# Three extension pairs instead of one, an x ring of 14 pieces, and LoRA factors held for one batch

## What is computed

```python
# conditioning: a dense layer plus the LoRA of the batch's slot
A, Bm = lora_As[adapter_mapping], lora_Bs[adapter_mapping]
c = einsum('bti,oi->bto', x, W) + b + einsum('btr,bro->bto', einsum('bti,bir->btr', x, A), Bm) * 2
# mixture of 8 experts of rank 16, the best one chosen by the router
logits = c @ route_w.T
topk_v, topk_idx = top_k(logits, 1)
route_weight = one_hot(topk_idx) * topk_v
h = einsum('bsd,erd->bser', c, Aexp)
return x + einsum('bser,eor->bso', route_weight[..., None] * h, Bw)
```

## Time and profile before

| | us |
|---|---|
| median of 3 runs | 283.86 |
| the profiled execution | 284.19 |
| its span | 282.4 |
| PE busy | 277.1 (98%) |
| DVE busy | 200.7 (71%) |
| ACT busy | 110.3 (39%) |
| DMA, share of 16 engines by q1 | 76.1% |

### The profile page before, as it was taken

The page is one execution under the profiler, slowest core; times in us unless marked ns, Lnnn a source line. Parts: engine busy times, 40 slices in busy tenths (PEclk is TensorE's granted clock), DMA queues, the critical chain, the costliest instruction groups (busy, mean ns, idle before and its releaser), DMA issues.

```text
span 282.4 us, 4103 instructions
## 1 busy us (share of the span) xinstructions
PE 277.1 (98%) x1601; PEld 221.0 (78%) x1601; DVE 200.7 (71%) x223; ACT 110.3 (39%) x151; POOL 14.9 (5%) x46
## 2 busy tenths in 40 slices
PE   8999999999999999999999999999999999999993
PEld 5999999997773888888588758867885888588882
DVE  0033010177497889999889969996998799788794
ACT  0001011387684645534275346326533743370000
POOL 7600021000001000000000000000000000000000
PEclk9999999999999999999999999999999999999999
DMA  7999999999993034999966993999399859606688
GB/s 257 382 377 394 399 407 411 384 407 421 412 408 133 2 149 187 352 343 388 396 269 230 418 402 146 348 405 398 136 370 406 316 176 412 287 22 253 261 355 321
DMA packets 19590, 88.50 MB, mean 313 GB/s; under 512 B 2410, under 2 KB 4594, under 8 KB 12018
## 3 DMA queue, kind: packets, MB, share of 16 engines
q1 hardware_dynamic: 16272, 83.70, 76.1%
q10 hardware_dynamic: 3298, 4.54, 4.4%
HBM read 54.60 MB, written 33.55 MB: 312 GB/s over the span
## 4 chain that ended last, share of the span: by engine, by line
PE 93%; DVE 6%; issue 0%; DVEq 0%
PE bank_out L683 11%; PE bank_eh L811 11%; PE bank_eh L825 10%; PE bank_eh L840 10%; PE bank_out L749 9%; PE bank_out L772 9%; PE bank_out L763 9%; PE bank_eh L683 5%; PE bank_rl L683 5%; PE bank_rl L790 5%; PE bank_eh L790 5%; DVE x_ring L666 4%; PE bank_rl L721 1%; PE bank_eh L711 1%; PE bank_rl L845 1%; PE bank_eh L846 1%
## 5 line engine op out<-in xcount | busy, mean ns | idle before, releaser
L402 ACT ACTIVATE x_hi<-x_ring 128x1024 fp32r<-128x1024 f32 x64 | 67.4, 1061 | 57.7 <-PE bank_eh L840 57.3
L518 DVE TENSOR_TENSOR x_lo<-x_ring,x_hi 128x1024 fp32r<-128x1024 f32 x64 | 77.6, 1222 | 8.7 <-ACT x_hi L402 8.7
L607 DVE TENSOR_TENSOR x_ring<-bank_out,x_ring 128x1024 f32<-128x1024 f32 x54 | 65.9, 1220 | 2.9 <-PE bank_out L772 2.7
L811 PE MATMUL bank_eh<-x_hi,m_hi 128*128 128x512 f32 x128 | 50.6, 396 | 0.0
L825 PE MATMUL bank_eh<-x_lo,m_hi 128*128 128x512 f32 x128 | 49.9, 390 | 0.0
L840 PE MATMUL bank_eh<-x_hi,m_lo 128*128 128x512 f32 x128 | 49.8, 389 | 0.0
L749 PE MATMUL bank_out<-wh_hi,bw_hi 128*128 128x512 f32 x120 | 46.7, 389 | 0.0
L763 PE MATMUL bank_out<-wh_lo,bw_hi 128*128 128x512 f32 x120 | 46.7, 389 | 0.0
L772 PE MATMUL bank_out<-wh_hi,bw_lo 128*128 128x512 f32 x120 | 46.7, 389 | 0.0
L811 PEld LDWEIGHTS bank_eh<-x_hi,m_hi 128*128 128x128 f32 x128 | 24.0, 188 | 10.7 <-issue 5.9
L840 PEld LDWEIGHTS bank_eh<-x_hi,m_lo 128*128 128x128 f32 x128 | 24.0, 188 | 5.1
(11 more groups left out here) (99 smaller groups left out, 227.1 us busy)
## 6 DMA issues: line engine op xcount, KB each, us to landing
x_ring<-xT SPq DMA_DIRECT2D x32, 1024.0 KB, 8.4
outT<-x_ring SPq DMA_DIRECT2D x26, 1024.0 KB, 4.9
w_ring<-W SPq DMA_DIRECT2D x24, 512.0 KB, 10.6
w_ring<-W SPq DMA_DIRECT2D x14, 256.0 KB, 5.9
outT<-x_ring SPq DMA_DIRECT2D x5, 512.0 KB, 2.8
outT<-x_ring ACTq DMA_DIRECT2D x4, 512.0 KB, 2.8
outT<-x_ring SPq DMA_DIRECT2D x5, 256.0 KB, 2.7
x_ring<-loraB ACTq DMA_DIRECT2D x8, 128.0 KB, 9.9
```

The costliest lines, as they stand in the source:

```text
L402: act.activation(out, in_, ACT.Copy).then_inc(done, 1)
L518: dve.tensor_tensor(out, a, b, ALU.subtract).then_inc(done, 1)
L607: dve.tensor_tensor(x, out_bank(b, j)[:, :, :], x, ALU.add).then_inc(v_out, 1)
L811: mm(bank_h, m_hi[:, c, :], hi, start=(c == 0), stop=False)
```

## The change

1. `TWINS = range(2, 7, 2)`: extensions 2, 4 and 6 now run straight after extensions 1, 3 and 5. ACT, DVE and PE treat 4 and 6 as they treated 2; PE's waits that belong to them move to the end of the batch two before.
2. `XRING` is 14 and `LAG` is 1: after `store(k)` comes `load_x(k + 13)`, which waits until store k - 1 has landed.
3. `la` holds one batch. Each `load_a(b)` waits until GpSimd has copied the factor before (`g_ext`); `load_a(1)` and `load_a(2)` stand among the ACT work of phase 1, `load_a(b + 3)` behind the `wh_hi` copy of batch b, up to b = 4.
4. Room for the ring: `g_a`, `bp`, `pb_sum`, `ones` and `bias_sb` lie in slot 10 (`WORK`), whose first load waits for their last readers; `e_top`/`e_two` and `e_odd`/`e_sum` share two tiles in different partitions. The two copies of `stack` change places.

```diff
-    XRING = 12
+    XRING = 14
...
+        TWINS = range(TWIN, NB - 1, 2)
...
                 if k >= XRING:
                     sp.wait_ge(d_out[slot], 16 * (k // XRING))
+                elif slot == WORK:
+                    sp.wait_ge(t_pb, 1)
+                    sp.wait_ge(v_glo, 3)
+                    sp.wait_ge(a_ghi, 6)
+                    sp.wait_ge(a_beats, 3)
...
-            LAG = 2
+            LAG = 1
...
             def load_ext(b):
-                if b == TWIN + 1:
-                    pool.wait_ge(d_la, 16 * (NB - TWIN - 1))
+                pool.wait_ge(d_la, 16 * (b + 1))
...
+            def load_a(b):
+                if b >= 1:
+                    act.wait_ge(g_ext, b)
+                act.dma_start(la[:, :, :].rearrange("p c r -> p (c r)"),
+                              loraA[bass.ds(slot[b], 1), :, :].rearrange("s p n -> p (s n)")).then_inc(d_la, 16)
...
                 copy(wh_hi[b % 2][:, :], wh[:, :], a_wh)
+                if b + 3 < NB:
+                    load_a(b + 3)
...
+                ext_last = b + 3 if b + 3 in TWINS else b + 2
...
-                        pe.wait_ge(g_ext, ext_next + 1)
+                        pe.wait_ge(g_ext, ext_last + 1)
...
-                    if (b, j, i) == (TWIN - 2, NP2 - 1, 1):
-                        pe.wait_ge(v_wh, TWIN)
+                    if b + 2 in TWINS and (j, i) == (NP2 - 1, 1):
+                        pe.wait_ge(v_wh, b + 2)
...
-                if b != TWIN:
+                if b not in TWINS:
                     extension(b)
-                if b + 1 == TWIN:
-                    extension(TWIN)
+                if b + 1 in TWINS:
+                    extension(b + 1)
```

More of the change, by code:

```diff
@@ L107, in adaln_ffn, with work @@
         x_ring = sb("x_ring", [P, XRING, PIECE])
-        lb = x_ring[:, 8, :].rearrange("p (b c r) -> p b c r", b=NB, c=C)
-        bw_raw = x_ring[:, 9, :]
+        lb = x_ring[:, 12, :].rearrange("p (b c r) -> p b c r", b=NB, c=C)
+        bw_raw = x_ring[:, 13, :]
         lb_cols = x_ring[:, 11, :].rearrange("p (c b r) -> p c b r", b=NB, c=C)
-        EARLY = (8, 9, 11)
+        EARLY = (11, 12, 13)
+        WORK = 10
+        def work(at, n, rows=P):
+            return x_ring[0:rows, WORK, at:at + n]
+        g_a = work(0, NB * XN, GROUP).rearrange("p (b n) -> p b n", b=NB)
+        bp = work(NB * XN, XN)
+        pb_sum = [work((NB + 1) * XN + i * PN, PN) for i in range(2)]
+        ones = work((NB + 1) * XN + 2 * PN, P)
+        bias_sb = work((NB + 1) * XN + 2 * PN + P, C)
+        assert (NB + 1) * XN + 2 * PN + P + C <= PIECE
         phase1 = ExitStack()
@@ L129, in adaln_ffn @@
         wh = sb("wh", [P, T])
[L130 to L136, removed]
+        assert (C - WO) * PN + NHEAD * (HEAD_W + HO * PN) + XN + 2 * E + P // 2 <= 7 * T, "the second lot covers the first"
+        e_st = sb("e_st", [P, T], F32R)
+        ahead = sb("ahead", [P, T], F32R)
+        e_bias = sb("e_bias", [P, 1])
         slots = sb("slots", [1, NB], I32)
+        sb("space", [P, HALF - 16])
         m_hi = sb("m_hi", [P, C, ER], F32R)
@@ L443, in _ @@
                     act.dma_start(g_a[BIAS_ROW:BIAS_ROW + 1, :, :], pb[:, :].unsqueeze(1).broadcast_to([1, NB, XN])).then_inc(d_g, 16)
+                    load_a(1)
                 if n == NWB - 2:
@@ L459, in _ @@
                         split_hi(0, j)
+                    load_a(2)
                 m_block(blk)
-            load_a(TWIN + 1, NB)
             def top(b):
@@ L479, in stack @@
                     act.wait_ge(t_stack, b)
+                copy(e_st[2 * GROUP:3 * GROUP, :], e_sum[:, :], a_ehi)
                 copy(e_st[0:GROUP, :], e_sum[:, :], a_ehi)
-                copy(e_st[2 * GROUP:3 * GROUP, :], e_sum[:, :], a_ehi)
             for b in range(NB):
-                if b != TWIN:
+                if b not in TWINS:
                     top(b)
                 for j in range(NP2):
-                    if j == 0 and b != TWIN:
+                    if j == 0 and b not in TWINS:
                         odd(b)
-                    if b + 1 == TWIN and j == 0:
+                    if b + 1 in TWINS and j == 0:
                         stack(b)
[L491 to L496, removed]
+                        top(b + 1)
+                    if b + 1 in TWINS and j == 1:
+                        odd(b + 1)
+                    if b + 1 in TWINS and j == TWIN_AT:
+                        stack(b + 1)
+                    if j == EHI_AT and b not in TWINS and b + 1 not in TWINS:
                         stack(b)
@@ L640, in _ @@
                         split_lo(b, SRING + j)
-                    elif b + 1 < NB and (b + 1, j) != (TWIN, NP2 - 1):
+                    elif b + 1 < NB and not (b + 1 in TWINS and j == NP2 - 1):
                         split_lo(b + 1, j - SRING)
@@ L742, in out_pair @@
                     pe.wait_ge(v_whlo, b + 1)
-                ext_next = b + 2 if j == NP2 - 1 and TWIN < b + 2 < NB else None
+                ext_next = b + 2 if j == NP2 - 1 and TWIN < b + 2 < NB and b + 2 not in TWINS else None
+                ext_last = b + 3 if b + 3 in TWINS else b + 2
                 hi, lo = wh_hi[b % 2][:, :], wh_lo[b % 2][:, :]
@@ L787, in extension @@
                             pe.wait_ge(v_m, NWB)
-                        if c == C - 1 and b > TWIN:
+                        if c == C - 1 and b > TWIN and b not in TWINS:
                             pe.wait_ge(v_wh, b)
```

58 lines of the change are left out of this document (24 added, 34 removed).

## The result

| | before | after |
|---|---|---|
| median of 6 runs | 283.87 us (283.49 to 284.16) | 288.88 us (288.06 to 289.87) |
| ratio, 95% interval | 1 | 1.0174 (1.0161 to 1.0188) |
| profiled execution | 284.19 us | 288.40 us, span 286.6 us |

A forecast was written before the change was run, and what follows sets the result against it. PE, busy 98% of the span, was taken to bound the kernel. On the profiled 284.19 us, -0.70 (pairs) + 2.3 + 1.2 (waits) = +2.8 us: 287.0 us profiled, 286.7 us median; range 283.1 to 288.6 us.

The forecast's parts named there:

- Late arrivals are paid in full: On PE, busy 98% of the span: whatever arrives late adds its whole delay, since PE has no idle time.
- A pair saves 0.35 us: On PE, two extensions back to back save one entry into and exit from the 32-column form; two new pairs save 0.70 us.
- First wait, 2.3 us: In extension 4, PE waits for x piece 19, landing at 144.0 us against a deadline of 141.76 us.
- its turn comes no later: Piece 19's load, issued 1.5 us later by the lag, stands behind store 6 either way, so no delay was added.
- Second wait, 1.2 us: In the pair of extensions 5 and 6, PE waits for piece 27; the middle between 0 and 2.3 us.
- The cause, one fetch packet that a full queue can't make good: A PE program fetch on queue q8 at 124 us delays the full DMA queue by 2.1 us; landings take 9.4, not 7.0.
- The factor load, 0.3 us: `load_a(5)`, 0.13 MB on ACT's queue, mixes packets with piece 19's load and makes it 0.3 us later.
- What costs nothing: Factor loads on ACT, copies at batch ends, slot 10's late first load and PE's waits for `v_wh` add no time.
- (a): Rival: all pieces in time, loads landing in 7.0 + 0.3 us, only the 0.70 us saving stays; 283.2 us, chance 20%.
- (b): Rival: only the fetch packet's own 1.3 us counts, landings near 8.0, waits 0.7 us in all; 283.9 us, chance 12%.
- (c): Rival: ACT held in phase 1 by `load_a(2)`, extension 0 waits some 1.2 us; 287.9 us on the forecast, chance 5%.
- (d): Rival: the late load is issued and lands later, waits 3.8 us at first pair, 2.3 at second; 289.3 us, chance 6%.

The follow-up runs named there:

- e3: The changed kernel, but extensions 4 and 6 read the x pieces of batches 3 and 5, already there, so the output differs; 283.08 us.
- e2: The changed kernel with only the pairs of extensions (1, 2) and (3, 4), without the pair (5, 6); 286.92 us.
- e1: The changed kernel with only the old pair, extensions 1 and 2; ring of 14, lag of 1 and factor loads stay; 283.91 us.
- e6: The changed kernel with LAG = 2, so every load comes one store later; 300.64 us.
- e5: The changed kernel with 96 extra PE instructions in phase 1 that wait for nothing, so the fetch packets fall elsewhere; 287.44 us.
- e8: The changed kernel without the factor loads of batches 3 to 7, whose extensions use factor 2, so the output differs; 287.12 us.
- e10: The changed kernel with factor loads half a batch later and 96 extra PE instructions in phase 1 that move the fetch packets; 286.11 us.
- e12: The changed kernel with factor loads half a batch later, loads 19 and 27 ahead of stores 6 and 14, and 96 extra PE instructions; 284.35 us.
- e9: The changed kernel with the factor loads issued half a batch later, same computation; 286.59 us.

## Why the prediction was off, point by point

- *Late arrivals are paid in full.* Right: +4.1 us by the losses, +4.2 measured between the profiled executions. Of the signs, the landings "over 9 us" came true for the first load only (9.3, then 8.5 and 8.7 us), since the others left later than I had them.
- *A pair saves 0.35 us.* Right: 52.11 us against 52.46 from pair A to pair B, 7.00 us per pair wherever nothing is late, and e3 is 0.8 to 1.0 us under the kernels with one pair.
- *First wait, 2.3 us.* Right to 0.1 (2.43), with luck in it. The load left at 135.75 and not 134.32, because it waited for store 5, as my upper end had it; and it took 8.7 us and not 9.7, because "its turn comes no later" was nearly right as well. It landed at 144.45, 0.45 us later than I had it (in e2, the same program up to there, at 144.09, so most of that is scatter), and PE could do without it until 142.02 (144.45 - 2.43), 0.26 us later than my deadline of 141.76. The two differences cancel for the most part.
- *Second wait, 1.2 us.* **This is the term that failed**: 2.34 us. I took the middle between "all in time" and "as the first", because the packet would come 1.4 us sooner and might fall in a gap. It came no sooner: it stands at 179.2 us, 11.4 ahead of its pair, and the first at 124.6, 11.5 ahead of its own. The 12 instructions behind the 1.4 us had no footing, for my own rows have 275 from one packet to the next in one stretch and 262 in the other. Nor did it find a gap: the 16 engines' share was 1.01 from 178 to 190 us, and the loads of 172.8, 178.4, 183.7 and 189.3 took 7.9, 8.4, 9.5 and 9.6 us. Stretches alike in load should have been given the same delay. The middle of two ends is not a value when one of the ends has no mechanism.
- *The cause, one fetch packet that a full queue can't make good.* Supported, as the start: moved, it gave back 1.36 and 0.99 us. 1.1 and 1.4 us were left, with a packet beside the late loads again. The Trainium skill ("Runtime: NRT & Kernel Launch", Instruction fetch mechanics) calls the cost of crossing such a block mostly hidden. For PE's own run this case's trace agrees (in after it is busy 16.00 of the 16.00 us from 120 to 136 us, with the packet in them); for the loads that share the engines it doesn't, as moving the packet away gave back 1.0 to 1.4 us.
- *The factor load, 0.3 us.* Too small at the second pair: 0.8 us, and about 0.4 at the first.
- *What costs nothing.* Right: e1 equals before, with the ring, slot 10 and the loads on ACT in it. Extension 0 started at 68.53 us, 0.1 later than before.
- *Rivals.* (a) needed a landing under 7.4 us; the late loads took 8.7 and 9.6. The 6.8 us that I estimated for a store and a load from the Trainium skill ("DMA: Bandwidth & Descriptors", Anatomy of one DMA) is met only by the loads next to a pause (6.9 to 7.0 us in after, too); the page fits its formula to single transfers on GpSimd's path, while these go by SP. (b) fell with the result: it needed landings near 8.0 and waits of 0.7 us in all, and the losses are 4.77. (c) did not happen. (d) was half right: the load was issued 1.4 us later but landed only 0.45 later. Its 289.3 us lies nearest to the measured time, but by terms (3.8 and 2.3 us) that were not measured.
- *The median.* I took off 0.33 us from the profiled execution, as before. After's median lies 0.48 us above its profile: 0.8 us of the miss of 2.2; the second wait is 1.1 of it, the first 0.1. With a second wait of 2.34 us the forecast would have been 287.8 us, inside the range; it is this term, taken over from the kernel before as if fixed, that puts the time above it. Its cause is open (last section).

## What to carry to other kernels

Where a stream fills the DMA engines and the engine that bounds the kernel has no gap, moving a consumer one piece ahead of its loads costs what the queue is behind at that place, not what the median transfer takes; look at the transfer that stands there, and give every stretch of the same load the same delay. Look for what shares the queue beside the late transfer (a store nobody waits for, a small load with half a batch to spare, program fetches) and put the late one ahead: two loads put ahead of a store, and later factor loads, turned +1.7% into -0.2%. And ask what stands behind a wait on an in-order queue before shortening a lag: the step from 1 to 0 cost 30 us.

## What the runs showed of the hardware

**TensorE's clock fell after long waits.** In e6 PE stood for 2.79 us, worked, and stood for 3.89 us; the granted clock was 0.90 from 144 to 145 us, 0.50 (the level of 1.2 GHz) from 145 to 151, and back at 1.00 from 152 on. The main product's first matmuls started 0.59, 0.43 and 0.41 us apart there instead of 0.34 and 0.23. In the profiled execution of after, with waits of 2.2 us, it stayed at 1.00. But four of its six runs had a mean of 0.994 and took 288.79 to 289.87 us; the two with 1.000 took 288.06 and 288.40. If the clock stood at half, 0.006 of 287 us is an estimated 3.4 us at the lower level. That these lie behind the new waits was not seen, as those runs have no profile. The experiments with waits of 0.5 to 1.6 us show the same: in e5 284.82 us at a mean of 1.000 and 288.31 and 288.92 at 0.994 and 0.992; in e8 287.07 at 1.000 and 288.33 at 0.992; in e10 285.47 at 1.000 and 288.33 at 0.994. In e1 and e3, without such waits, no run is under 0.996 and the time doesn't go by the clock. The clock isn't all of it: e12's profile has no such wait, and its three longest runs have means of 1.000, 0.993 and 0.989. This also spreads the medians of e5, e9 and e10, whose single terms are better read from the losses.

**A small load on a second queue can cost a large one more than its bytes.** 128 KB of factors beside the late load made it about 0.4 us later at pair A and 0.8 at pair B, with 0.39 us of engine time for its packets; only at B is that more than the bytes and the packets account for.

**Full engines don't move bytes at a steady rate.** In after the 16 engines had a share of 1.00 from 181 to 182 us and moved 279 GB/s, and of 0.99 from 184 to 185 us and moved 401. The kernel before has such dips as well (295 GB/s at a share of 1.10 from 120 to 121 us), so they don't separate the kernels; what makes them is open.
